# Graph attention layer: two heads' features in the two halves of the array, denominators as products of 32 columns

## The chip, the core and the metric

The kernel runs on one core of a Trainium2 chip. The metric is the device time of one execution in microseconds (us). TensorE multiplies, VectorE (DVE), ScalarE (ACT) and GpSimd (POOL) work element by element, and SyncE (SP) issues most transfers.

## What is computed

Four layers of a graph network run one after the other on 3125 nodes of 256 features. The change touches only the last one, graph attention with 4 heads of 64 features:

```python
ft = (feat @ W.T).reshape(n, HEADS, OUT_DIM)
a1 = jnp.einsum('nhd,hd->nh', ft, attn_l)
a2 = jnp.einsum('nhd,hd->nh', ft, attn_r)
e = jax.nn.leaky_relu(a1[src] + a2[dst], negative_slope=ALPHA)
m = jax.ops.segment_max(e, dst, num_segments=n)
ex = jnp.exp(e - m[dst])
s = jax.ops.segment_sum(ex, dst, num_segments=n)
msg = ft[src] * (ex / s[dst])[:, :, None]
out = jax.ops.segment_sum(msg, dst, num_segments=n)
return jax.nn.elu(out.reshape(n, HEADS * OUT_DIM))
```

For every head and target node this is a weighted sum of 64 features over the sources, and one more sum, of the weights alone, by which it is divided.

## The kernel before

Earlier layers build a dense matrix of edge counts, 25 by 25 blocks of 128 by 128 in bf16. The attention layer (`l3_fast`, from L2015) uses it in place of gathers. The targets are cut into ranges of up to 7 blocks (`RANGES`), and the layer runs 9 passes (`PASSES`, L1924), each for one pair of heads `i` and one range: four ranges for heads 0 and 1, five for heads 2 and 3. A pass has 25 steps `k`, one for each block of 128 sources.

In a step, for each head `u` of the pair, VectorE makes a tile of weights `wgt` (L2185), 128 sources by all targets of the range, in fp32, from the counts `cj`, a row `ratio` and a scalar for each source. TensorE multiplies it (L2234): the stationary operand is `ftx[:, k, head, :]`, 65 columns, which are 64 features and a column of scale factors whose product is the denominator; the moving operand is `wgt`. A range of more than 512 targets is cut into two pieces. So a step of a wide pass has 4 matmuls in the program, 2 heads by 2 pieces, and the five-block or smaller range has 2. Each fp32 matmul of the program appears in the trace as two weight loads and two matmuls on the same columns and the same output. They accumulate in `acc[p % 2][u]`, 65 partitions of two PSUM banks for each head; two passes alternate.

`wgt` has `NW = 3` buffers. VectorE waits for `m`, which TensorE raises after each head's matmuls (L2236), and TensorE waits for `w`. When a pass ends, ScalarE copies the accumulators to `oT` (L2109), TensorE turns them back at step 3 of the next pass (`turn`, L2214), and VectorE divides at its step 6 (`divide`, L2131) and, for the second pair of heads, applies the end of the layer (L2153 to L2164). GpSimd and VectorE scale `ftx` once ahead of the first pass (L2085, L2127). In the first pass TensorE also turns 25 small blocks (`row`, L2204).

Of the kernel before, what the change touches and what calls it, by code (L numbers as in the profile page):

```python
# [19 lines left out]
P = 128  # L20
N = 3125
# [1993 lines left out]
def l3_fast(nc, sem, sb, a, f, out):  # L2015
# [8 lines left out]
    with ExitStack() as ctx:  # L2024
        def buf(name, shape, dt=F32):
            return sb(name, shape, dt, ctx)
        NW, NC, FIRST = 3, 4, 3
        MOST = RANGES[0][1]
        UPPER = [p for p, (i, r) in enumerate(PASSES) if i]
        qs, e2, ng = buf("l3q", [P, NT, H]), buf("l3e2", [P, NT, H]), buf("l3ng", [P, H])  # L2030
# [1 line left out]
        rb = buf("ratio", [P, H, NP])  # L2032
        wgt = buf("wgt", [P, NW, 2, MOST * P])
        cj = buf("fcj", [P, NC, MOST, P], BF16)
        oT = buf("oT", [P, 2, MOST * P])
        den, rden = buf("fden", [P, 2, MOST]), buf("frden", [P, 2, MOST])
        neg = buf("fneg", [P, MOST, D])
        o = hx[:, :, 0:D]
        acc = [[psum[:, 4 * b + 2 * u:4 * b + 2 * u + 2, :] for u in range(2)] for b in range(2)]
        pR = psum[:, 4:6, :]  # L2040
        width = lambda r: min(N, (RANGES[r][0] + RANGES[r][1]) * P) - RANGES[r][0] * P
        half = lambda r: -(-width(r) // 2)
        pieces = lambda r: [(0, width(r))] if width(r) <= 512 else [(0, half(r)), (half(r), width(r))]
        span = lambda r: slice(RANGES[r][0], RANGES[r][0] + RANGES[r][1])
        ROWS_AT, TURN_AT, DIVIDE_AT, FINISH_AT, STORE_AT = 6, 3, 6, 10, 16
        WIDE_AT = (17, 20)
# [34 lines left out]
        @block.gpsimd  # L2081
        def _(eng):
            eng.wait_ge(s_("exp"), 2)
            for k in range(FIRST, NT):
                eng.tensor_tensor(ftx[:, k, :, :], ftx[:, k, :, :], e2[:, k, :].unsqueeze(2).to_broadcast([P, H, FW]), ALU.mult)\  # L2085
                   .then_inc(s_("ft"), 1)

        @block.scalar
        def _(eng):
            eng.wait_ge(s_("z"), 1)  # L2090
            eng.activation(qs[:, :, :], rr[:, :, 0:H], ACT.Exp, scale=0.8).then_inc(s_("exp"), 1)  # L2091
            eng.activation(e2[:, :, :], rr[:, :, 0:H], ACT.Exp, scale=0.2).then_inc(s_("exp"), 1)
            nt = RANGES[0][1]
            for u in range(2):
                eng.activation(rb[:, u, 0:nt * P], acc[0][u].rearrange("p b n -> p (b n)")[:, 0:nt * P], ACT.Exp,  # L2095
                               bias=ng[:, u:u + 1], scale=-0.8).then_inc(s_("rbp"), 1)
            eng.activation(rr[:, :, H:2 * H], rr[:, :, H:2 * H], ACT.Exp, scale=-0.8).then_inc(s_("exp"), 1)
            for g in range(7):
                w = min(4, NT - 4 * g) * P
                eng.wait_ge(s_("rowed"), g + 1)  # L2100
                eng.activation(rsb[:, 4 * g * P:4 * g * P + w], pR[0:H, g % 2, 0:w], ACT.Copy).then_inc(s_("rows"), 1)
            for p, (i, r) in enumerate(PASSES):
                nb = len(pieces(r))
                n = pieces(r)[0][1]
                eng.wait_ge(s_("m"), 2 * NT * (p + 1))
                if p:
                    eng.wait_ge(s_("turned"), p)
                for u in range(2):
                    last = eng.activation(oT[0:FW, u, 0:nb * n].rearrange("p (b n) -> p b n", b=nb), acc[p % 2][u][0:FW, 0:nb, 0:n], ACT.Copy)  # L2109
                    last.then_inc(s_("oT"), 1)  # L2110
                if i:
                    eng.wait_ge(s_("neg"), UPPER.index(p) + 1)
                    eng.activation(neg[:, 0:RANGES[r][1], :], neg[:, 0:RANGES[r][1], :], ACT.Exp).then_inc(s_("elu"), 1)

        @block.vector
        def _(eng):
# [7 lines left out]
            eng.wait_ge(s_("exp"), 2)  # L2124

            def scaled(k):
                eng.tensor_tensor(ftx[:, k, :, :], ftx[:, k, :, :], e2[:, k, :].unsqueeze(2).to_broadcast([P, H, FW]), ALU.mult)\  # L2127
                   .then_inc(s_("ft_first"), 1)
            scaled(0)

            def divide(p):  # L2131
# [2 lines left out]
                short = t0 + nt == NT  # L2134
                whole = nt - 1 if short else nt
                eng.wait_ge(s_("turned"), p + 1)
                sums = [acc[p % 2][u][:, 0, 0:nt * FW].rearrange("p (t f) -> p t f", f=FW) for u in range(2)]
                parts = [(P, 0, whole)] + ([(N - (NT - 1) * P, whole, nt)] if short else [])
                for u in range(2):
                    for q, lo, hi in parts:  # L2140
                        ch.do(eng.tensor_scalar(den[0:q, u, lo:hi], sums[u][0:q, lo:hi, HD], 1e-37, None, ALU.max))  # L2141
                ch.after()
                for q, lo, hi in parts:
                    ch.do(eng.reciprocal(rden[0:q, :, lo:hi], den[0:q, :, lo:hi]))  # L2144
                ch.after()
                for u in range(2):
                    for q, lo, hi in parts:
                        ch.do(eng.tensor_tensor(o[0:q, t0 + lo:t0 + hi, HD * (2 * i + u):HD * (2 * i + u + 1)], sums[u][0:q, lo:hi, 0:HD],  # L2148
                                                rden[0:q, u, lo:hi].unsqueeze(2).to_broadcast([q, hi - lo, HD]), ALU.mult))
                ch.after()  # L2150
                eng.sem_inc(s_("ev"), 1)
                if i:
# [13 lines left out]
            for p, (i, r) in enumerate(PASSES):  # L2166
# [4 lines left out]
                for k in range(NT):  # L2171
# [8 lines left out]
                    for u in range(2):  # L2180
                        if n == 0:
                            eng.wait_ge(s_("rbp"), u + 1)
                        if n >= NW:
                            eng.wait_ge(s_("m"), 2 * (n - NW) + u + 1)
                        eng.scalar_tensor_tensor(out=wgt[:, n % NW, u, 0:w], in0=rb[:, 2 * i + u, t0 * P:t0 * P + w],  # L2185
                                                 scalar=qs[:, k, 2 * i + u:2 * i + u + 1],
                                                 in1=here.rearrange("p k d -> p (k d)")[:, 0:w],
                                                 op0=ALU.max, op1=ALU.mult).then_inc(s_("w"), 1)
# [6 lines left out]
        def _(eng):  # L2195
# [11 lines left out]
            def turn(p):  # L2207
                r = PASSES[p][1]
                t0, nt = RANGES[r]
                eng.wait_ge(s_("oT"), 2 * p + 2)  # L2210
                for u in range(2):
                    for t in range(nt):
                        q = min(P, N - (t0 + t) * P)
                        last = eng.transpose(acc[p % 2][u][0:q, 0, t * FW:(t + 1) * FW], oT[0:FW, u, t * P:t * P + q], ident[0:FW, 0:FW])  # L2214
                last.then_inc(s_("turned"), 1)
            for p, (i, r) in enumerate(PASSES):
                if p == 1:
                    eng.wait_ge(s_("rows"), 7)
                if p > 1:
                    eng.wait_ge(s_("ev"), p - 1)  # L2220
                for k in range(NT):
# [6 lines left out]
                        eng.wait_ge(s_("ft_first"), k + 1)  # L2228
                    elif p == 0:
                        eng.wait_ge(s_("ft"), k - FIRST + 1)  # L2230
                    for u in range(2):
                        eng.wait_ge(s_("w"), 2 * n + u + 1)
                        for b, (lo, hi) in enumerate(pieces(r)):
                            last = eng.matmul(acc[p % 2][u][0:FW, b, 0:hi - lo], ftx[:, k, 2 * i + u, :], wgt[:, n % NW, u, lo:hi],  # L2234
                                              start=k == 0, stop=k == NT - 1, skip_group_check=True)
                        last.then_inc(s_("m"), 1)  # L2236
            turn(len(PASSES) - 1)


# [281 lines left out]
```

## Time and profile before

| | |
|---|---|
| median of 3 runs | 2154.23 us (2144.46 to 2157.07) |
| the profiled execution, its own time | 2139.71 us |
| its span, first to last instruction | 2137.8 us |
| mean granted clock of TensorE | 0.914 |
| span of the attention layer's 9 passes, first to last of the L2234 matmuls | 1582.0 to 2121.5 us |

In the trace "PE" is TensorE's matmuls, "PEld" its weight loads, and Ln is a line of the kernel. A matmul's duration includes the way through the array, so durations of successive matmuls overlap; the distance between two starts, called a slot here, is what each costs in a row of them. The same holds for VectorE to a smaller degree. "Busy" in the tables counts overlapped time once, "mean ns" does not.

### The profile page before, as it was taken

What the parts mean: (1) busy time and instruction counts of PE and PEld (TensorE: products, weight loads), DVE (VectorE), ACT (ScalarE), POOL (GpSimd) and SP (SyncE); (2) the same over time, 40 slices, a digit from 0 to 9 for tenths busy, and PEclk for the clock granted to TensorE, in tenths of its full rate; (3) what the DMA queues carried; (4) which work ended last, traced back from release to release, by engine and by line L of the source; (5) the groups of instructions that cost most, each with busy time, mean ns of one, the idle gap of its engine ahead of it and who ended that gap; (6) DMA issues with size and microseconds to landing.
All of it is one profiled execution on the core that took longest, in us unless ns stands there. A gap on an engine that the chain in (4) does not pass through costs nothing. (4 is left out here: it accounts for less than half of the span.)

```text
span 2137.8 us, 22846 instructions
## 1 busy us (share of the span) xinstructions
PE 1862.9 (87%) x7207; PEld 1136.3 (53%) x7207; DVE 1305.1 (61%) x1926; ACT 507.0 (24%) x738; POOL 1078.9 (50%) x1646
## 2 busy tenths in 40 slices
PE   3868967789979888988766999999889999999996
PEld 1246742266656555656554756778753444434443
DVE  5976758845524343443423565665587788878887
ACT  0500020034543434434333534200240000000000
POOL 3888888888888888888888700000032000000000
PEclk8955569899999999999888999999899999999998
DMA  9788850015544534443423432487223333434432
GB/s 352 316 323 338 323 187 23 9 36 182 185 138 140 167 110 156 151 155 135 143 93 139 155 114 81 147 300 227 93 48 91 89 81 86 102 89 106 96 83 69
DMA packets 335681, 313.04 MB, mean 146 GB/s; under 512 B 274432, under 2 KB 320234, under 8 KB 325867
## 3 DMA queue, kind: packets, MB, share of 16 engines
q1 hardware_dynamic: 220153, 265.90, 36.8%
q10 hardware_dynamic: 89654, 45.29, 7.2%
q0 software_dynamic: 25792, 0.88, 1.0%
q8 instruction: 36, 0.59, 0.1%
q14 instruction: 46, 0.38, 0.1%
HBM read 180.44 MB, written 131.55 MB: 146 GB/s over the span
## 5 line engine op out<-in xcount | busy, mean ns | idle before, releaser
L409 POOL DMA_INDIRECT table<-valT,idxT x806 | 777.5, 965 | 174.7 <-issue 139.9
L2234 PE MATMUL psum<-wgt,big 128*65 128x384 f32 (+4 forms) x1600 | 530.7, 493 | 8.6 <-DVE wgt L2185 8.5
L2185 DVE SCALAR_TENSOR_TENSOR wgt<-ratio,l3q,fcj 128x768 f32<-128x768 f32 (+4 forms) x442 | 408.0, 947 | 90.1 <-PE psum L2234 84.1
L2234 PEld LDWEIGHTS psum<-wgt,big 128*65 128x65 f32 x1600 | 219.4, 138 | 310.6 <-issue 283.9
L905 PE MATMUL psum<-hx,region 128*128 128x257 f32 x1250 | 303.9, 388 | 35.8 <-issue 28.5
L905 PE MATMUL psum<-region,g 128*128 128x512 f32 (+1 forms) x672 | 282.5, 566 | 1.5 <-DVE big L683 1.5
L905 PEld LDWEIGHTS psum<-hx,region 128*128 128x128 f32 x1250 | 229.7, 193 | 77.7 <-issue 39.5
L683 DVE TENSOR_TENSOR big<-big,psum 128x512 f32<-128x512 f32 (+1 forms) x325 | 209.5, 664 | 96.3 <-PE psum L905 65.4
L407 POOL MEMSET rest<- 128x256 f32 x805 | 264.4, 328 | 1.1 <-DMA table<-valT,idxT 0.6
L905 PEld LDWEIGHTS psum<-region,g 128*128 128x128 f32 x672 | 124.5, 195 | 126.7 <-issue 109.8
L1153 POOL PARTITION_ALL_REDUCE edges<-edge x1 | 0.5, 515 | 351.9 <-DVEq L1530 351.9
L849 ACT ACTIVATE region<-psum 128x512 f32<-128x512 f32 (+1 forms) x175 | 90.9, 551 | 357.3 <-PE psum L1004 250.9
L905 PE MATMUL psum<-tk,hx 128*128 128x100 bf16 x806 | 146.2, 357 | 22.2 <-DVE tk L629 21.4
L1238 PE MATMUL psum<-l2both,l2z 128*128 128x512 f32 (+1 forms) x700 | 147.6, 371 | 3.3 <-DVE l2z L1419 3.3
L905 PEld LDWEIGHTS psum<-tk,hx 128*128 128x128 bf16 x806 | 115.4, 145 | 52.7 <-DVE tk L629 24.7
L1004 PE MATMUL psum<-ident,tk 128*128 128x128 f32 x625 | 99.1, 292 | 47.7 <-DMA tk<-table 46.8
L1238 PEld LDWEIGHTS psum<-l2both,l2z 128*128 128x128 f32 x700 | 128.1, 189 | 22.2 <-DVE l2z L1419 4.1
L1385 DVE TENSOR_TENSOR l2both<-l2m 128x2560 fp32r<-128x2560 bf16 (+1 forms) x35 | 88.8, 2537 | 65.4 <-PE psum L1238 59.7
L1004 PEld LDWEIGHTS psum<-ident,tk 128*128 128x128 f32 x625 | 94.0, 206 | 52.9 <-DMA tk<-table 47.4
L2109 ACT ACTIVATE oT<-psum 65x768 f32<-65x768 f32 (+4 forms) x18 | 12.4, 741 | 449.5 <-PE psum L2234 449.5
L528 DVE TENSOR_TENSOR big<-psum,big 128x2048 bf16<-128x2048 f32 x48 | 109.4, 2289 | 12.6 <-ACT psum L801 7.9
L686 DVE TENSOR_TENSOR region<-region,ident 128x128 f32 (+1 forms) x24 | 7.0, 293 | 159.5 <-ACT region L874 154.5
(250 smaller groups left out, 1656.6 us busy)
## 6 DMA issues: line engine op xcount, KB each, us to landing
table<-tk SPq DMA_DIRECT2D x25, 3200.0 KB
tk<-table SPq DMA_DIRECT2D x25, 1664.0 KB
tk<-table SPq DMA_DIRECT2D x25, 1536.0 KB
fcj<-counts_b SPq DMA_DIRECT2D x125, 192.0 KB, 2.6
counts_t<-region ACTq DMA_DIRECT2D x25, 800.0 KB
counts_b<-region ACTq DMA_DIRECT2D x25, 800.0 KB
table<-valT,idxT POOLq DMA_INDIRECT x806
l2m<-counts_b SPq DMA_DIRECT2D x20, 640.0 KB, 5.4
```

Of the source, the lines that this page charges most:

```text
L407: eng.memset(rest[:, :], 0.0).then_inc(sem("rest"), 1)
L409: eng.indirect_dma_start(out=table, out_offset=bass.IndirectOffsetOnAxis(idxT[:, c:c + 1], 0), in_=valT[:, c, :], in_offset=None).then_inc ...
L528: eng.tensor_tensor(out, kbp[:, s, :].unsqueeze(1).unsqueeze(1).to_broadcast([P, 2, SB, P]), overlap(win[:, s, :, SB * m:SB * m + P]), ALU ...
L683: eng.tensor_tensor(part, part, more, ALU.add).then_inc(sem("af"), 1)
L849: eng.activation(cs[:, 4 * g:4 * g + w, :].rearrange("p j d -> p (j d)"), pC[:, g % 3, 0:w * P], ACT.Copy)\
L905: mm = lambda o, l, r_, st, sp: eng.matmul(o, l, r_, start=st, stop=sp, skip_group_check=True)
L1004: last = eng.transpose(pC[:, g % 3, o:o + P], tk[:, s, j, :, 0], ident[:, :])
L1238: mm = lambda o, l, r_, st, sp: eng.matmul(o, l, r_, start=st, stop=sp, skip_group_check=True)
L1385: eng.tensor_tensor(all_of(both[:, n % 2, :, :, :]), all_of(ca[n % NB]), all_of(cb[n % NB]), ALU.add).then_inc(s_("sum"), 1)
L2109: last = eng.activation(oT[0:FW, u, 0:nb * n].rearrange("p (b n) -> p b n", b=nb), acc[p % 2][u][0:FW, 0:nb, 0:n], ACT.Copy)
L2185: eng.scalar_tensor_tensor(out=wgt[:, n % NW, u, 0:w], in0=rb[:, 2 * i + u, t0 * P:t0 * P + w], scalar=qs[:, k, 2 * i + u:2 * i + u + 1], ...
L2234: last = eng.matmul(acc[p % 2][u][0:FW, b, 0:hi - lo], ftx[:, k, 2 * i + u, :], wgt[:, n % NW, u, lo:hi], start=k == 0, stop=k == NT - 1, ...
```

## The change

The two heads of a pass are multiplied on disjoint columns of the array: 64 features of head 0 write partitions 0 to 63, those of head 1 partitions 64 to 127 of the same bank (`product`). The denominators are no longer a 65th column. They are products of their own (`total`): the stationary operand is one column of scale factors repeated 32 times, and each of the four combinations of head and piece writes a quarter of 32 partitions of one bank, `sums`. `total` is called in every second step, for that step and the one before, and once alone in step 24. The banks, the copies (`oT` and a new `dT`), the transposes and the division follow the new layout, the pieces are cut at whole blocks, and `NW` goes from 3 to 5, since `m` now rises only after `total`. The scaling of `ftx` leaves the 65th column out. The wait for `rows` at pass 1 goes, since `pR` has banks of its own.

```diff
-        NW, NC, FIRST = 3, 4, 3
+        NW, NC, FIRST = 5, 4, 3
...
-        oT = buf("oT", [P, 2, MOST * P])
+        oT, dT = buf("oT", [P, MOST * P]), buf("dT", [P, 4 * P])
...
-        acc = [[psum[:, 4 * b + 2 * u:4 * b + 2 * u + 2, :] for u in range(2)] for b in range(2)]
-        pR = psum[:, 4:6, :]
+        flat = lambda t: t.rearrange("p b n -> p (b n)")
+        acc = [psum[:, 3 * b:3 * b + 2, :] for b in range(2)]
+        sums = [psum[:, 3 * b + 2, :] for b in range(2)]
+        scores_at = [flat(psum[:, 2 * u:2 * u + 2, :]) for u in range(2)]
+        pR = psum[:, 6:8, :]
-        half = lambda r: -(-width(r) // 2)
-        pieces = lambda r: [(0, width(r))] if width(r) <= 512 else [(0, half(r)), (half(r), width(r))]
+        half = lambda r: (RANGES[r][1] + 1) // 2
+        pieces = lambda r: [(0, width(r))] if width(r) <= 512 else [(0, half(r) * P), (half(r) * P, width(r))]
...
-                eng.tensor_tensor(ftx[:, k, :, :], ftx[:, k, :, :], e2[:, k, :].unsqueeze(2).to_broadcast([P, H, FW]), ALU.mult)\
+                eng.tensor_tensor(ftx[:, k, :, 0:HD], ftx[:, k, :, 0:HD], e2[:, k, :].unsqueeze(2).to_broadcast([P, H, HD]), ALU.mult)\
...
-                for u in range(2):
-                    last = eng.activation(oT[0:FW, u, 0:nb * n].rearrange("p (b n) -> p b n", b=nb), acc[p % 2][u][0:FW, 0:nb, 0:n], ACT.Copy)
-                    last.then_inc(s_("oT"), 1)
+                for bank, (lo, hi) in enumerate(pieces(r)):
+                    eng.activation(oT[:, lo:hi], acc[p % 2][:, bank, 0:hi - lo], ACT.Copy).then_inc(s_("oT"), 1)
+                eng.activation(dT[:, 0:n], sums[p % 2][:, 0:n], ACT.Copy).then_inc(s_("dT"), 1)
...
-                sums = [acc[p % 2][u][:, 0, 0:nt * FW].rearrange("p (t f) -> p t f", f=FW) for u in range(2)]
+                first = -(-pieces(r)[0][1] // P)
+                feats = flat(acc[p % 2])[:, 0:nt * P].rearrange("p (t u f) -> p t u f", u=2, f=HD)
+                totals = sums[p % 2].rearrange("p (t u b c) -> p b u t c", u=2, b=2, c=P // 4)
                 parts = [(P, 0, whole)] + ([(N - (NT - 1) * P, whole, nt)] if short else [])
-                for u in range(2):
+                for bank in range(len(pieces(r))):
                     for q, lo, hi in parts:
-                        ch.do(eng.tensor_scalar(den[0:q, u, lo:hi], sums[u][0:q, lo:hi, HD], 1e-37, None, ALU.max))
+                        lo, hi = max(lo, bank * first), min(hi, bank * first + first)
+                        if lo < hi:
+                            ch.do(eng.tensor_scalar(den[0:q, :, lo:hi], totals[0:q, bank, :, lo - bank * first:hi - bank * first, 0], 1e-37, None, ALU.max))
                 ch.after()
                 for q, lo, hi in parts:
                     ch.do(eng.reciprocal(rden[0:q, :, lo:hi], den[0:q, :, lo:hi]))
                 ch.after()
-                for u in range(2):
-                    for q, lo, hi in parts:
-                        ch.do(eng.tensor_tensor(o[0:q, t0 + lo:t0 + hi, HD * (2 * i + u):HD * (2 * i + u + 1)], sums[u][0:q, lo:hi, 0:HD],
-                                                rden[0:q, u, lo:hi].unsqueeze(2).to_broadcast([q, hi - lo, HD]), ALU.mult))
+                for q, lo, hi in parts:
+                    ch.do(eng.tensor_tensor(o[0:q, t0 + lo:t0 + hi, 2 * HD * i:2 * HD * i + 2 * HD].rearrange("p t (u f) -> p t u f", u=2), feats[0:q, lo:hi, :, :],
+                                            rden[0:q, :, lo:hi].rearrange("p u t -> p t u").unsqueeze(3).to_broadcast([q, hi - lo, 2, HD]), ALU.mult))
                 ch.after()
                 eng.sem_inc(s_("ev"), 1)
...
                         if n >= NW:
-                            eng.wait_ge(s_("m"), 2 * (n - NW) + u + 1)
+                            eng.wait_ge(s_("m"), 2 * (n - NW) + 2)
                         eng.scalar_tensor_tensor(out=wgt[:, n % NW, u, 0:w], in0=rb[:, 2 * i + u, t0 * P:t0 * P + w],
...
             def turn(p):
                 r = PASSES[p][1]
                 t0, nt = RANGES[r]
-                eng.wait_ge(s_("oT"), 2 * p + 2)
-                for u in range(2):
-                    for t in range(nt):
-                        q = min(P, N - (t0 + t) * P)
-                        last = eng.transpose(acc[p % 2][u][0:q, 0, t * FW:(t + 1) * FW], oT[0:FW, u, t * P:t * P + q], ident[0:FW, 0:FW])
+                r = PASSES[p][1]
+                eng.wait_ge(s_("oT"), sum(len(pieces(PASSES[e][1])) for e in range(p + 1)))
+                for t in range(nt):
+                    q = min(P, N - (t0 + t) * P)
+                    eng.transpose(flat(acc[p % 2])[0:q, t * P:(t + 1) * P], oT[:, t * P:t * P + q], ident[:, :])
+                eng.wait_ge(s_("dT"), p + 1)
+                n = pieces(r)[0][1]
+                for lo in range(0, n, P):
+                    last = eng.transpose(sums[p % 2][0:min(P, n - lo), lo:lo + P], dT[:, lo:min(n, lo + P)], ident[:, :])
                 last.then_inc(s_("turned"), 1)
+
+            def product(p, k):
+                i, r = PASSES[p]
+                for bank, (lo, hi) in enumerate(pieces(r)):
+                    for u in range(2):
+                        eng.matmul(acc[p % 2][HD * u:HD * u + HD, bank, 0:hi - lo], ftx[:, k, 2 * i + u, 0:HD], wgt[:, (NT * p + k) % NW, u, lo:hi],
+                                   start=k == 0, stop=k == NT - 1, skip_group_check=True)
+
+            def total(p, steps):
+                i, r = PASSES[p]
+                for k in steps:
+                    for u in range(2):
+                        for bank, (lo, hi) in enumerate(pieces(r)):
+                            at = P // 4 * (2 * u + bank)
+                            last = eng.matmul(sums[p % 2][at:at + P // 4, 0:hi - lo], e2[:, k, 2 * i + u:2 * i + u + 1].to_broadcast([P, P // 4]),
+                                              wgt[:, (NT * p + k) % NW, u, lo:hi], start=k == 0, stop=k == NT - 1, skip_group_check=True)
+                last.then_inc(s_("m"), 2 * len(steps))
             for p, (i, r) in enumerate(PASSES):
-                if p == 1:
-                    eng.wait_ge(s_("rows"), 7)
...
-                    for u in range(2):
-                        eng.wait_ge(s_("w"), 2 * n + u + 1)
-                        for b, (lo, hi) in enumerate(pieces(r)):
-                            last = eng.matmul(acc[p % 2][u][0:FW, b, 0:hi - lo], ftx[:, k, 2 * i + u, :], wgt[:, n % NW, u, lo:hi],
-                                              start=k == 0, stop=k == NT - 1, skip_group_check=True)
-                        last.then_inc(s_("m"), 1)
+                    eng.wait_ge(s_("w"), 2 * n + 2)
+                    product(p, k)
+                    if k % 2:
+                        total(p, (k - 1, k))
+                    elif k == NT - 1:
+                        total(p, (k,))
             turn(len(PASSES) - 1)
```

Not shown: ScalarE's first reads of the scores go by `scores_at`, the same banks as before, and the second scaling line (L2127) changes as the first.

## Rows read from the trace of the kernel before

**Rows 1.** The page's part 1, TensorE's entry: busy us, share, instructions.

```profile
PE 1862.9 (87%) x7207; PEld 1136.3 (53%) x7207; DVE 1305.1 (61%) x1926; ACT 507.0 (24%) x738; POOL 1078.9 (50%) x1646
```

**Rows 2.** Chain that ended last, from 1575 us to the end: shares by line.

```profile
by line: PE psum L2234 90.3%; DVE wgt L2185 2.0%; PE psum L2214 1.1%; issue 0.7%; DVE xs L2156 0.7%; DVE xs L2164 0.6%; DVE fneg L2153 0.5%; PE psum L2204 0.5%; DVE hx L2148 0.4%; ACT ratio L2095 0.2%; DVE fden L2141 0.1%; ACT oT L2109 0.1%
```

**Rows 3.** Windows: a wide pass (384 targets a piece), then the two narrow ones.

```profile
core 0: us, PE busy (x) PEld busy (x) DVE busy (x) ACT busy (x) POOL busy (x), PEclk, DMA share, GB/s
...
1662.00:1727.30 65.30, 65.30 (x215) 28.42 (x214) 52.17 (x55) 1.72 (x2) 0.00 (x0) 1.00 0.37 87
...
2058.40:2093.80 35.40, 33.42 (x113) 14.35 (x112) 32.65 (x58) 2.99 (x3) 0.00 (x0) 1.00 0.41 100
2093.80:2121.70 27.90, 26.85 (x107) 13.82 (x105) 24.79 (x54) 1.71 (x3) 0.00 (x0) 1.00 0.36 86
```

**Rows 4.** Groups by form, 1580 to 2138 us: the product's matmuls (347 is as 346).

```profile
L2234 PE MATMUL psum<-wgt,big 128*65 128x384 f32 x900 | 291.8, 486 | 2.0 <-DVE wgt L2185 2.0
...
L2234 PE MATMUL psum<-wgt,big 128*65 128x448 f32 x400 | 154.2, 545 | 5.5 <-DVE wgt L2185 5.5
...
L2234 PE MATMUL psum<-wgt,big 128*65 128x346 f32 x100 | 37.4, 455 | 0.0
...
L2234 PE MATMUL psum<-wgt,big 128*65 128x309 f32 x100 | 26.8, 424 | 1.1 <-DVE wgt L2185 0.9
```

**Rows 5.** Timeline of TensorE, a few matmuls of each width: start, us, instruction.

```profile
1699.43 1.45 PE L2234 MATMUL psum<-wgt,big 128*65 128x384 f32 x4
...
1879.72 1.67 PE L2234 MATMUL psum<-wgt,big 128*65 128x448 f32 x4
...
1819.78 1.62 PE L2234 MATMUL psum<-wgt,big 128*65 128x346 f32 x5
...
2109.76 1.46 PE L2234 MATMUL psum<-wgt,big 128*65 128x309 f32 x5
```

**Rows 6.** Timeline around 1701 us: two weight loads one slot apart.

```profile
1701.37 0.14 PEld L2234 LDWEIGHTS psum<-wgt,big 128*65 128x65 f32 x1 [0.18 <-issue]
1701.69 0.14 PEld L2234 LDWEIGHTS psum<-wgt,big 128*65 128x65 f32 x1 [0.18 <-issue]
```

**Rows 7.** Waits, 1582 to 2122 us: who for whom, us in total, times, longest.

```profile
DVE wgt L2185 <- PE psum L2234: 84.1, 277, 0.9
...
PE psum L2234 <- DVE wgt L2185: 8.5, 4, 5.5
```

**Rows 8.** Groups, 1580 or 1582 to 2138 us: VectorE's weight tiles (442 and 8).

```profile
L2185 DVE SCALAR_TENSOR_TENSOR wgt<-ratio,l3q,fcj 128x768 f32<-128x768 f32 x200 | 200.8, 1017 | 45.8 <-PE psum L2234 45.3 <-DVE hx L2148 0.4
...
L2185 DVE SCALAR_TENSOR_TENSOR wgt<-ratio,l3q,fcj 128x768 f32<-128x768 f32 (+4 forms) x442 | 408.0, 947 | 90.1 <-PE psum L2234 84.1 <-DMA fcj<-counts_b 4.1 <-DVE hx L2148 0.9
...
L2185 DVE SCALAR_TENSOR_TENSOR wgt<-ratio,l3q,hx 128x896 f32<-128x896 f32 x8 | 9.8, 1279 | 0.5 <-ACT ratio L2095 0.5
```

**Rows 9.** Timeline of VectorE, three weight tiles made without a wait between them.

```profile
1943.72 2.87 DVE L2185 SCALAR_TENSOR_TENSOR wgt<-ratio,l3q,fcj 128x768 f32<-128x768 f32 x3
```

**Rows 10.** Groups of VectorE, 1582 to 2138 us: its larger work beside the weights.

```profile
L2148 DVE TENSOR_TENSOR hx<-psum,frden 128x384 f32<-128x384 f32 (+5 forms) x22 | 8.9, 453 | 0.3
...
L2156 DVE SCALAR_TENSOR_TENSOR xs<-hx,xs 128x1536 f32<-128x1536 f32 (+2 forms) x5 | 7.5, 1492 | 0.8 <-DVE fneg L2153 0.8
L2164 DVE SCALAR_TENSOR_TENSOR xs<-fneg,xs 128x1536 f32<-128x1536 f32 (+2 forms) x5 | 7.4, 1487 | 0.0
L2153 DVE TENSOR_SCALAR fneg<-hx 128x1536 f32<-128x1536 f32 (+2 forms) x5 | 5.8, 1169 | 0.7
```

**Rows 11.** Timeline of TensorE in the first pass: small transposes between products.

```profile
1602.26 0.60 PE L2204 MATMUL psum<-ident,small 128*4 128x128 f32 x4
1602.70 3.17 PE L2234 MATMUL psum<-wgt,big 128*65 128x448 f32 x8
```

**Rows 12.** The chain in order of time (start, us, what), around a turn.

```profile
1670.02 0.87 PE psum L2214 x14
1670.89 64.50 PE psum L2234 x200
```

More of the change, by code:

```diff
@@ L2094, in _ @@
             for u in range(2):
-                eng.activation(rb[:, u, 0:nt * P], acc[0][u].rearrange("p b n -> p (b n)")[:, 0:nt * P], ACT.Exp,
+                eng.activation(rb[:, u, 0:nt * P], scores_at[u][:, 0:nt * P], ACT.Exp,
                                bias=ng[:, u:u + 1], scale=-0.8).then_inc(s_("rbp"), 1)
@@ L2102, in _ @@
             for p, (i, r) in enumerate(PASSES):
-                nb = len(pieces(r))
                 n = pieces(r)[0][1]
@@ L2126, in scaled @@
             def scaled(k):
-                eng.tensor_tensor(ftx[:, k, :, :], ftx[:, k, :, :], e2[:, k, :].unsqueeze(2).to_broadcast([P, H, FW]), ALU.mult)\
+                eng.tensor_tensor(ftx[:, k, :, 0:HD], ftx[:, k, :, 0:HD], e2[:, k, :].unsqueeze(2).to_broadcast([P, H, HD]), ALU.mult)\
                    .then_inc(s_("ft_first"), 1)
```

## Prediction, made before the kernel with the change was run

> **What bounds the kernel now.** I read the page's busy times first, then the chain of waits for the stretch of the attention layer, then that stretch by windows, groups and timeline. TensorE is the busiest engine of the whole kernel, 87% [rows 1]. In the stretch that the change touches, from 1575 us to the end, 90.3% of the chain is the matmuls of L2234 and only 2.0% VectorE's weight tiles [rows 2]. In a wide pass TensorE is busy for all of 65.30 us and VectorE for 52.17, at a granted clock of 1.00, which is 2.4 GHz [rows 3]. VectorE waits 84.1 us for those matmuls, in 277 waits, and TensorE only 8.5 us for VectorE, in four [rows 7]. So TensorE's slots set the length of the layer, and VectorE is the next limit.
>
> What a slot is: four matmuls of 384 columns take 1.45 us, one of them 0.486 [rows 4, 5], so a start follows a start after (1.45 - 0.486) / 3 = 0.321 us. In the same way 448 columns cost (1.67 - 0.545) / 3 = 0.375, 346 cost (1.62 - 0.455) / 4 = 0.291, and 309 cost (1.46 - 0.424) / 4 = 0.259 us. A weight load starts one slot after the one before it and lasts 0.14 us [rows 6], so it lies under a running matmul and costs nothing.
>
> The layer in slots: 900 x 0.321 + 400 x 0.375 + 200 x 0.291 + 100 x 0.259 = 288.9 + 150.0 + 58.2 + 25.9 = 523 us. 100 of the 900 and the 100 of 309 columns are the two narrow passes, 58 us; the seven wide passes have 1400 matmuls, 465 us. The layer's matmuls run from 1582.0 to 2121.5 us, 539.5 us, so 16.5 us is starts, transposes and waits. All sums are made against the profiled execution's own 2139.7 us; the median of the runs shown is 14.5 us above it, and I add what I find to the median.
>
> **The change part by part.**
>
> *How many matmuls.* The width of the stationary operand does not enter a slot: 65 columns take 0.321 us for 384 moving columns, which is 2 x 384 clocks at 2.4 GHz and nothing for the 65. So 64 columns cost the same, and the separate denominators double the number: 2800 in the wide passes for 1400, 400 in the narrow ones for 200. In series that would be 523 us more. All now depends on how much of it runs at the same time on different columns of the array, and no row of before has two matmuls at once. The bounds are one at a time, 523 us more, and as many as there are disjoint column ranges, two in `product` and four in `total`.
>
> *What I take for the overlap.* Each fp32 matmul of the program is two in the trace, on the same columns (A A', then for the other head B B'). A' needs A's columns, so it starts one slot after A. In the rows every matmul starts after the one before it in program order. If TensorE keeps to that order, B cannot pass the waiting A', and starts with it. Then B' and the next A start together, and so on: a chain in which two run at once, never more, and whose end adds one slot. For `product` of two wide steps, 16 matmuls, that gives 8 + 1 slots. For `total` of the same two steps, again 16 matmuls in pairs, on four quarters in turn, it gives also 8 + 1, since the third quarter is blocked behind the second half of the second just as well. Before, two steps took 16 slots. So with an order that is kept the four quarters bring no more than the two halves, and the work per slot is exactly what it was.
>
> *The end of each group.* Whether the 1 is paid depends on whether halves and quarters may run at once. Below: not at all, if the quarters start as soon as their columns are free; then `total` begins in the slot in which `product`'s last pair ends, and nothing is lost. The nearest rows are the first pass's small transposes: four of them and then eight products start without a gap [rows 11], but these all use the array as one piece. Above: the array runs empty at each change, then the chain's extra slot is paid and the matmul's way out too, 0.486 - 0.321 = 0.165 us, and at worst a weight load of 0.14 us that nothing covers. I take the extra slot and the way out without the load, since the halves and quarters are different divisions of the same columns and the load can be under way while the last matmul drains. The Trainium skill says so of the first part (TensorEngine Tiling (Array Packing), Tiling Modes, Key Properties): a change of the tiling mode, not of the tile alone, drains TensorE. By it the sum is the one below; without it this item is zero. No run here shows it yet.
>
> *The sum.* A wide pass: twelve pairs of steps at 18 slots and the last step at 5 + 5, 226 slots for 200, so 0.13 x 465 = +60.5 us. A narrow pass has 8 matmuls in `product` of two steps, so 5 + 5 for 8, and 3 + 3 for the last step: 126 for 100, 0.26 x 58 = +15.1 us. Changes between halves and quarters: 13 groups x 2 x 9 passes = 234, at 0.165 us +38.6 us.
>
> *The small parts.* `turn` has 11 transposes for 14 (7 + 4) in the first pass, but their moving side is 128 wide: four such take 0.44 us [rows 11], 0.11 each, so 1.2 us where 14 now take 0.87 [rows 12]; nine passes give about +2.3 us. The copies on ScalarE cover fewer columns and lie beside the next pass's matmuls, except the last; the division has fewer instructions and is off the path while VectorE has room. In the two narrow passes 35.4 + 27.9 = 63.3 us [rows 3] stand against 58 of slots: VectorE's divisions hold TensorE there; a slower TensorE hides about 3 us of it, -3. `NW = 5` covers the later release: two buffers belong to the pair that runs, three more steps are ready, and VectorE refills two in 4 x 0.93 = 3.7 us, while TensorE takes 18 slots, 5.8 us. The wait for both heads' weights in place of one is hidden for the same reason, as is the coarser `m`. The scaling of `ftx` and the wait for `rows` are at most some tenths of a us.
>
> Together 60.5 + 15.1 + 38.6 + 2.3 - 3 = +113.5 us: 2139.7 + 113.5 = 2253 for a profiled execution, and 2154.2 + 113.5 = 2268 as a median. With the uncovered loads it is 234 x 0.138 = 32 more, 2300.
>
> **The rivals.**
>
> *A, full overlap, faster.* TensorE holds a waiting matmul for each range of columns, so that B starts with A and all four quarters run at once. A pair of wide steps is then 8 + 4 slots, a wide pass 150 for 200: -0.25 x 465 = -116 us. A narrow pass has only two quarters in use and is even. With the drains (38.6) and `turn` it is -75, 2079 us. Without the drains TensorE would ask for 2154 - 114 = 2040, but now VectorE stops it. Its 442 tiles x 0.947 + 8 x 1.279 = 429 us [rows 8] less an overlap of 1.017 - (2.87 - 1.017) / 2 = 0.09 each [rows 9], so 389 us, with 29.6 us of the rows beside [rows 10] and some 5 us of small ones: 423 us for 539.5. Since each pass goes by the slower of the two, I take about -105, 2049 us. For it speaks that disjoint columns share nothing but the order; against it that every start in the trace follows program order. It decides from the point at which a pair of steps takes less than 16 slots with its drains. The Trainium skill (TensorE: Matmul & The Clock Gate, Part 3, Measured speedup vs the span model) gives 2.38 times for three column tiles; taken over to both parts that would be this rival. The same part says that matmuls start and end strictly in order, which is my forecast's side. Neither measured two in a row on one tile.
>
> *B, order kept but no drain: no change.* 16 slots for 16, with +2.3 and some stalls hidden: 2154 us, 2140 to 2165. For it: the rows without a gap [rows 11].
>
> *C, little or no overlap, much slower.* If weight loads wait for the column range before them, each A to B passage shows a load; if nothing overlaps, the layer costs 523 us more, 2677 us. Anything above 2300 is here.
>
> **How the numbers follow.** Forecast 0.37 (2230 to 2300), A 0.34 (2040 to 2085), B 0.14, C 0.13, rest 0.02. The forecast is the likeliest, 2268. The range 2040 to 2300 leaves out C and the rest; it holds both signs, the forecast's own is 2230 to 2300. About 1% is what a measurement can tell from no change: faster 0.34, same 0.15, slower 0.51.
>
> **What would show it.** In the profile after, the timeline of a wide pass: starts of matmuls in pairs, one slot between pairs, in both lines, and after each group a gap of about 0.165 us and no start for a slot; 5.8 to 6.1 us for two steps where 5.15 stand now; VectorE waiting for TensorE more than 84 us. Four starts within 0.02 us in `total` would refute the order and give A. `product`'s last and `total`'s first matmul side by side give B. Starts never together give C. If VectorE is busy without a wait in the wide passes, the layer is near A's lower end.

## The result and the profile after

The kernel with the change takes 2086.94 us (median of 4 runs, 2078.43 to 2087.63), the kernel before 2149.35 us beside it (4 runs). The ratio is 0.9701, with a 95% interval of 0.9652 to 0.9749: 3% faster, some 62 us. The forecast was 2268 us and slower. Rival A, full overlap, had 2079 us with the drains, and a range of 2040 to 2085.

Windows of the changed kernel, over the same three passes as [rows 3] (columns as there) and one pass of the second pair of heads:

```profile
1669.10:1722.60 53.50, 53.50 (x413) 19.45 (x411) 48.48 (x55) 1.47 (x3) 0.00 (x0) 1.00 0.46 108
...
1890.30:1946.50 56.20, 54.05 (x413) 19.25 (x411) 53.72 (x58) 3.17 (x4) 0.00 (x0) 1.00 0.49 118
...
2001.00:2039.40 38.40, 37.48 (x213) 11.36 (x209) 31.85 (x57) 2.74 (x4) 0.00 (x0) 1.00 0.39 96
2039.50:2070.80 31.30, 30.93 (x208) 11.13 (x206) 23.75 (x50) 1.75 (x4) 0.00 (x0) 1.00 0.31 73
```

The wide pass of 65.30 us is now 53.50, with twice the matmuls (x413 for x215) and the same granted clock. The narrow passes went the other way, 38.4 + 31.3 for 35.4 + 27.9 us. The layer's matmuls run from 1600.3 to 2070.3 us: 470.0 us for 539.5, 69.5 less.

The span of this profiled execution is only 51.9 us shorter (2085.9 for 2137.8), since the layer began 18 us later, at 1600.3 for 1582.0. No run shows that the change does this: in the seven runs below on chips of like speed the layer begins between 1588 and 1600 us, and in the one of them that is the kernel before with more buffers at 1599.3.

Timeline of TensorE, changed kernel, inside the second pass (start, us, instruction):

```profile
1691.41 2.80 PE L2230 MATMUL psum<-wgt,big 128*64 128x384 f32 x16
1694.14 1.50 PE L2239 MATMUL psum<-wgt,l3e 128*32 128x384 f32 x16
1695.57 2.80 PE L2230 MATMUL psum<-wgt,big 128*64 128x384 f32 x16
1698.30 1.50 PE L2239 MATMUL psum<-wgt,l3e 128*32 128x384 f32 x16
```

A pair of steps repeats every 1695.57 - 1691.41 = 4.16 us. From the first of the 16 products to the first of the next line it is 2.73 us, which is two at a time (8 slots are 2.58), and for the 16 denominators' products 1.43 us, four at a time (4 slots are 1.29). So what is beyond 12 slots, 3.87 us, is 0.29 us, or 0.145 on average for each change between halves and quarters. In the single records the products start in pairs, 6 to 7 ns apart, the second pair 0.374 us after the first and each further one 0.322 us after the one before, and the denominators in fours, again 6 to 7 ns from one to the next.

Groups by form, changed kernel:

```profile
L2230 PE MATMUL psum<-wgt,big 128*64 128x384 f32 x1200 | 224.5, 495 | 3.6 <-DVE wgt L2190 3.4
...
L2239 PE MATMUL psum<-wgt,l3e 128*32 128x384 f32 x1200 | 150.1, 492 | 0.0
```

The waits of the layer, changed kernel (who for whom, us, times, longest):

```profile
PEld psum L2230 <- DVE wgt L2190: 62.0, 102, 1.7
...
DVE wgt L2190 <- PE psum L2239: 29.1, 51, 1.8
...
PE psum L2230 <- DVE wgt L2190: 10.5, 10, 6.6
DVE fden L2147 <- PE psum L2223: 10.1, 9, 5.5
```

One matmul of 384 columns still lasts about 0.49 us, as in [rows 4]. What changed is how many run at once. VectorE waits 29.1 us for TensorE's products instead of the 84.1 of [rows 7], and TensorE's loads now wait 62.0 us for VectorE. Before, that was 15.5 us:

```profile
PEld psum L2234 <- DVE wgt L2185: 15.5, 54, 2.1
```

A waiting load costs nothing while matmuls run. In the wide pass of 53.50 us TensorE is still busy all the time, and VectorE for 48.48; in the second pair's pass of 56.20 us VectorE is busy for 53.72, and TensorE, with 54.05, has gaps. So TensorE still sets the first pair's passes, with VectorE close behind, and VectorE's extra work in the second pair's now holds TensorE up.

### The profile page after: what moved, and what is told of

It is laid out like the page before. It is cut to its first block and busy times, and to the rows that moved or that the text cites. A ratio compares the mean times of both kernels' runs of the same rounds, so it can differ in the third digit from the quotient of the medians.

```text
span 2085.9 us, 25985 instructions
## 1 busy us (share of the span) xinstructions
PE 1769.4 (85%) x8777; PEld 1080.1 (52%) x8786; DVE 1285.5 (62%) x1911; ACT 502.8 (24%) x745; POOL 1082.0 (52%) x1646
## 3 DMA queue, kind: packets, MB, share of 16 engines
q1 hardware_dynamic: 220153, 265.90, 37.6%
## 5 line engine op out<-in xcount | busy, mean ns | idle before, releaser
L2190 DVE SCALAR_TENSOR_TENSOR wgt<-ratio,l3q,fcj 128x768 f32<-128x768 f32 (+4 forms) x442 | 388.2, 950 | 35.4 <-PE psum L2239 29.1
L2230 PE MATMUL psum<-wgt,big 128*64 128x384 f32 (+2 forms) x1600 | 294.2, 502 | 10.8 <-DVE wgt L2190 10.5
L905 PE MATMUL psum<-region,g 128*128 128x512 f32 (+1 forms) x672 | 270.1, 547 | 1.0 <-DVE big L683 1.0
L1004 PE MATMUL psum<-ident,tk 128*128 128x128 f32 x625 | 106.3, 308 | 173.2 <-DMA tk<-table 172.4
L905 PEld LDWEIGHTS psum<-hx,region 128*128 128x128 f32 x1250 | 235.8, 197 | 31.7 <-ACT region L849 0.6
L2230 PEld LDWEIGHTS psum<-wgt,big 128*64 128x64 f32 x1600 | 103.4, 137 | 196.1 <-issue 127.8
L1004 PEld LDWEIGHTS psum<-ident,tk 128*128 128x128 f32 x625 | 99.4, 208 | 180.2 <-DMA tk<-table 174.3
L2239 PE MATMUL psum<-wgt,l3e 128*32 128x384 f32 (+2 forms) x1600 | 176.2, 497 | 0.0
L905 PEld LDWEIGHTS psum<-tk,hx 128*128 128x128 bf16 x806 | 116.1, 144 | 37.9 <-DVE tk L629 10.1
## 6 DMA issues: line engine op xcount, KB each, us to landing
tk<-table SPq DMA_DIRECT2D x25, 1664.0 KB, 10.1
```

What stands on the lines that cost most here:

```text
L905: mm = lambda o, l, r_, st, sp: eng.matmul(o, l, r_, start=st, stop=sp, skip_group_check=True)
L1004: last = eng.transpose(pC[:, g % 3, o:o + P], tk[:, s, j, :, 0], ident[:, :])
L2230: eng.matmul(acc[p % 2][HD * u:HD * u + HD, bank, 0:hi - lo], ftx[:, k, 2 * i + u, 0:HD], wgt[:, (NT * p + k) % NW, u, lo:hi], start=k == ...
L2239: last = eng.matmul(sums[p % 2][at:at + P // 4, 0:hi - lo], e2[:, k, 2 * i + u:2 * i + u + 1].to_broadcast([P, P // 4]), wgt[:, (NT * p + ...
```

## The experiments

The number to compare is the layer's, from its first matmul to its last, in one profiled execution each: 539.5 us before, 470.0 with the change. Seven runs were on chips on which the kernel before takes 2146 to 2156 us. The other five (the products in rows of eight, the denominators on halves, the later division, the narrow passes and the last one) were on chips on which it takes 2332 to 2333 us, so their whole times are only comparable with the kernel before beside them; with 384 columns the rhythm of the changed code, 4.157 us, is the same there. Where no ratio is given, the kernel was timed in one execution only, and the argument goes by its rhythm and its layer.

### Which order do the matmuls start in

The forecast rested on this. Two runs alter the order in which the program gives the matmuls.

> The changed kernel with one edit: in a step, head 0's matmuls for both pieces come ahead of head 1's, where they alternated by head. Theory P (parking): a matmul whose columns are busy is set aside, one for each range of columns, and the next in program order goes on; only a second one for the same columns blocks. Then head 1 lags head 0 by two slots at the start of each product, and a pair of wide steps takes 10 + 4 slots for 8 + 4: with 384 columns a period of 4.157 + 0.645 = 4.80 us, the layer about 470 + 45 = 515 us. Theory D (deep): many wait for each range of columns: the period stays 4.157 us and the layer 470 us. Theory O (strict order, with the two passes of the fp32 matmul interleaved by head in the instruction stream): four in a row on the same columns run one by one, no pair starts together within a step, period about 16 slots for the product, 6.7 us, layer over 600 us.

```diff
-                for bank, (lo, hi) in enumerate(pieces(r)):
-                    for u in range(2):
+                for u in range(2):
+                    for bank, (lo, hi) in enumerate(pieces(r)):
                         eng.matmul(acc[p % 2][HD * u:HD * u + HD, bank, ...
```

> The changed kernel with one edit: in the denominators' products the two steps are the innermost loop, so that four matmuls of the trace in a row go to one quarter, then four to the next. Theory P: each quarter lags the one before by two slots, 10 slots for 4, period 4.157 + 6 x 0.322 = 6.1 us. Theory D: 4 slots as now, period 4.157 us. Theory O: about one by one, 16 slots, 8 us.

```diff
-                for k in steps:
-                    for u in range(2):
-                        for bank, (lo, hi) in enumerate(pieces(r)):
+                for u in range(2):
+                    for bank, (lo, hi) in enumerate(pieces(r)):
+                        for k in steps:
```

Timeline of TensorE, head outermost:

```profile
1690.82 2.85 PE L2230 MATMUL psum<-wgt,big 128*64 128x384 f32 x16
1693.60 1.50 PE L2239 MATMUL psum<-wgt,l3e 128*32 128x384 f32 x16
1695.02 2.85 PE L2230 MATMUL psum<-wgt,big 128*64 128x384 f32 x16
```

The same, denominators in runs of four to one quarter:

```profile
1697.85 2.80 PE L2230 MATMUL psum<-wgt,big 128*64 128x384 f32 x16
1700.58 1.52 PE L2239 MATMUL psum<-wgt,l3e 128*32 128x384 f32 x16
1702.02 2.80 PE L2230 MATMUL psum<-wgt,big 128*64 128x384 f32 x16
```

The periods are 4.20 and 4.17 us where parking a single matmul would have given 4.80 and 6.1, and the layers 474.3 and 472.2 us. With four matmuls in a row for the same columns, those for other columns still start within the same slot: the quarters 13 to 14 ns apart instead of 6 to 7, the halves 13 to 14 ns at first and up to 57 ns towards the end of a line. Both the strict order of the forecast and the parking of one are out. The third run lengthens the row to eight.

> The changed kernel with the products of both steps of a pair made together, head 0's eight matmuls of the trace ahead of head 1's eight. Theory, a long list for each range of columns: the halves still run together, head 1 starts about 8 x 0.0065 = 0.05 us after head 0, a period of 4.2 to 4.3 us. If a list holds about four, head 1 lags by four slots and the period is 4.157 + 1.3 = 5.4 us. Beside this TensorE now starts the product only when the second step's weights are there, which costs up to 1.87 us a pair where VectorE is not ahead.

```diff
-                for bank, (lo, hi) in enumerate(pieces(r)):
-                    for u in range(2):
+                for u, k in [(u, k) for u in range(2) for k in steps]:
+                    for bank, (lo, hi) in enumerate(pieces(r)):
...
-                    product(p, k)
                     if k % 2:
+                        product(p, (k - 1, k))
                         total(p, (k - 1, k))
                     elif k == NT - 1:
+                        product(p, (k,))
                         total(p, (k,))
```

Timeline of the weight loads, one for each matmul, this kernel:

```profile
1883.68 0.19 PEld L2230 LDWEIGHTS psum<-wgt,big 128*64 128x64 f32 x2 [0.62 <-issue]
1884.06 0.14 PEld L2230 LDWEIGHTS psum<-wgt,big 128*64 128x64 f32 x1 [0.19 <-issue]
1884.38 0.14 PEld L2230 LDWEIGHTS psum<-wgt,big 128*64 128x64 f32 x1 [0.18 <-issue]
1884.70 0.14 PEld L2230 LDWEIGHTS psum<-wgt,big 128*64 128x64 f32 x1 [0.19 <-issue]
1885.03 0.84 PEld L2230 LDWEIGHTS psum<-wgt,big 128*64 128x64 f32 x7 [0.18 <-issue]
1886.05 0.14 PEld L2230 LDWEIGHTS psum<-wgt,big 128*64 128x64 f32 x1 [0.18 <-issue]
1886.38 0.14 PEld L2230 LDWEIGHTS psum<-wgt,big 128*64 128x64 f32 x1 [0.19 <-issue]
```

Timeline of its matmuls:

```profile
1883.68 4.14 PE L2230 MATMUL psum<-wgt,big 128*64 128x384 f32 x16
1887.76 1.50 PE L2239 MATMUL psum<-wgt,l3e 128*32 128x384 f32 x16
1889.18 4.14 PE L2230 MATMUL psum<-wgt,big 128*64 128x384 f32 x16
```

Here is the limit. Single loads, a slot apart, stand at the front, then seven within 0.84 us, which are those of both heads side by side, and single ones again at the end. A record does not name its head; by the order in the program, head 0's first four matmuls run alone, the fifth together with head 1's first, 5 ns apart, and head 1's last four alone. So head 1 lags by four slots, and the 16 products take 12 slots: 4.08 us to the next line for 2.73. The layer takes 581.1 us, 111 more than with the change. The period is 5.50 us, 4.157 + 4 slots + 0.05, as the expectation had for "about four". When the fifth starts, three are left for the same columns, and the program goes on past them; with seven left it had not. In the head-outermost run the three behind the first did not block either. So beside the running one, three may wait for the same columns. The count goes by range of columns and not by the whole: with the denominators in runs of four, the fourth quarter's first matmul starts 40 ns after the first quarter's, while nine others wait, three for each of the quarters ahead of it. Whether the limit counts matmuls or loads was not tried.

### Is it the overlap that saves the time

> The changed kernel with one edit: both heads' features are multiplied on partitions 0 to 63 (head 1's sums fall on head 0's, so the output is not the reference's). If overlap of the two halves is what saved the time, the product takes 16 slots for 8 and its starts come one by one, 0.322 us apart: a period of 4.157 + 2.58 = 6.7 us, the layer about 740 us. If the time came from the later release, the buffers or the narrower stationary operand, the layer stays near 470 us.

```diff
-                        eng.matmul(acc[p % 2][HD * u:HD * u + HD, bank, ...
+                        eng.matmul(acc[p % 2][0:HD, bank, ...
```

Timeline of TensorE:

```profile
1714.56 1.50 PE L2239 MATMUL psum<-wgt,l3e 128*32 128x384 f32 x16
1715.99 5.37 PE L2230 MATMUL psum<-wgt,big 128*64 128x384 f32 x16
1721.29 1.50 PE L2239 MATMUL psum<-wgt,l3e 128*32 128x384 f32 x16
```

Yes. With both heads on the same columns 16 products take 5.30 us for 2.73, the period is 6.73 us and the layer 725.3 us. Everything else is as in the changed kernel, so the two halves for the products alone are worth 255 us in it. The quarters still go four at a time.

### What a change between halves and quarters costs

> The changed kernel with one edit: the denominators' products come in every step, so halves and quarters change 50 times a pass and not 26. Theory: each change costs what the rhythm of the changed kernel shows, (4.157 - 12 x 0.322) / 2 = 0.145 us, whatever stands between. Then 24 more changes a pass, 216 x 0.145 = +31 us less what VectorE held back before: +25 to +31 us. Rival: a change costs nothing and the 0.29 us of a period is waiting for VectorE: 0 us.

```diff
-                    if k % 2:
-                        total(p, (k - 1, k))
-                    elif k == NT - 1:
-                        total(p, (k,))
+                    total(p, (k,))
```

> The changed kernel with the denominators' products on the two halves, 64 columns wide, in place of quarters (the sums of the two pieces of a wide pass fall on each other, so its output is not the reference's). The division of the array never changes. Theory: the gap of 0.416 us for a slot of 0.322 at each switch comes from the change of division and goes; the denominators take 8 slots for 4: a period of 16 x 0.322 = 5.15 us with 384 columns, the layer about 470 + 100 = 570 us. Rival: the gap comes from the other line's weights or bank and stays, period 5.4 us.

```diff
-                            at = P // 4 * (2 * u + bank)
-                            last = eng.matmul(sums[p % 2][at:at + P // 4, ...], e2[...].to_broadcast([P, P // 4]), ...
+                            at = HD * u
+                            last = eng.matmul(sums[p % 2][at:at + HD, ...], e2[...].to_broadcast([P, HD]), ...
```

Timeline of TensorE, denominators in every step:

```profile
1700.32 1.51 PE L2230 MATMUL psum<-wgt,big 128*64 128x384 f32 x8
1701.76 0.85 PE L2239 MATMUL psum<-wgt,l3e 128*32 128x384 f32 x8
1702.54 1.51 PE L2230 MATMUL psum<-wgt,big 128*64 128x384 f32 x8
```

The same, denominators on halves:

```profile
1861.26 2.80 PE L2239 MATMUL psum<-wgt,l3e 128*64 128x384 f32 x16
1863.84 2.80 PE L2230 MATMUL psum<-wgt,big 128*64 128x384 f32 x16
1866.42 2.80 PE L2239 MATMUL psum<-wgt,l3e 128*64 128x384 f32 x16
```

In every step the period is 2.22 us, 6 slots (1.93) and again 0.29 us for two changes. The layer is 496.4 us, +26.4 for 216 changes, which at 0.145 us are 31; that the rest had been waiting for VectorE before, as the expectation has it, is likely and not shown. With the array divided in one way only, a line follows the other after exactly 8 slots, 2.58 us, and the period is 5.16: nothing beyond the slots. So the 0.145 us belongs to the change of division and to nothing else. That layer is 546.0 us and not 570, because the changes that it saves were not in my round number: 50 slots more in each of seven wide passes are 116 us, 234 changes fewer 34, together +82 for the measured +76. A pair then takes 16 slots, as in the kernel before, whose layer was 539.5 us: halves for everything gain nothing, and the gain of the change lies in the quarters.

### The buffers

> The kernel before with five weight buffers for three and nothing else. TensorE set the pace in the wide passes and VectorE's extra lead covers only the divisions in the narrow ones: 0 to -3 us. If the buffers were a part of the gain, it would be -10 us or more.

```diff
-        NW, NC, FIRST = 3, 4, 3
+        NW, NC, FIRST = 5, 4, 3
```

> The changed kernel with three weight buffers for five. Two belong to the pair of steps that runs, so VectorE is one step ahead at most. It makes step k+1 while k's pair runs and the next two only after the denominators' products: TensorE waits about one step's weights, 1.87 us less the 1.29 us of a product, in each pair: +0.6 to +1.9 us in each of some 108 pairs, +60 to +150 us. Rival: VectorE's lead does not matter, 0 us.

```diff
-        NW, NC, FIRST = 5, 4, 3
+        NW, NC, FIRST = 3, 4, 3
```

The kernel before with five buffers: ratio 1.0002 (0.9979 to 1.0025), layer 538.9 us. By themselves they are worth nothing. The changed kernel with three: ratio to the kernel before 1.0097 (1.0059 to 1.0135), layer 567.6 us, 97.7 more than with five, inside the expected 60 to 150. Its timeline shows how:

```profile
1691.28 1.50 PE L2239 MATMUL psum<-wgt,l3e 128*32 128x384 f32 x16
1692.70 1.51 PE L2230 MATMUL psum<-wgt,big 128*64 128x384 f32 x8
1694.91 1.51 PE L2230 MATMUL psum<-wgt,big 128*64 128x384 f32 x8 [0.70 <-DVE wgt L2190]
1696.35 1.50 PE L2239 MATMUL psum<-wgt,l3e 128*32 128x384 f32 x16
```

One step's products, then 0.70 us idle for VectorE, then the second's. The products in pairs of steps need buffers that hold them: with three, the gain turns into a loss of 1%.

### What is left: fewer changes, the narrow passes, the division's place

> The changed kernel with the denominators' products in every third step (9 groups a pass for 13) and six buffers. Theory: 8 changes a pass fewer, 72 x 0.145 = 10 us; VectorE's own work is 423 us of the layer's 470, so it gives -5 to -10 us. Rival: VectorE holds TensorE already, 0 us.

```diff
-        NW, NC, FIRST = 5, 4, 3
+        NW, NC, FIRST = 6, 4, 3
...
-                    if k % 2:
-                        total(p, (k - 1, k))
+                    if k % 3 == 2:
+                        total(p, tuple(range(k - 2, k + 1)))
                     elif k == NT - 1:
-                        total(p, (k,))
+                        total(p, tuple(range(NT - NT % 3, NT)))
```

Ratio to the kernel before 0.9678 (0.9628 to 0.9728), layer 467.7 us: -2.3, less than the 5 to 10 expected. The period is 6.09 us for three steps, 2.03 for one instead of 2.08, so in the steady rhythm TensorE got what was due, and the rest went elsewhere. The trace also shows a wait that grew:

```profile
DVE fden L2147 <- PE psum L2223: 22.4, 9, 5.0
DVE wgt L2190 <- PE psum L2239: 16.5, 25, 1.9
```

VectorE comes to the division before TensorE has turned the sums: 22.4 us for 10.1. One wait of each, 5.0 and 5.5 us, is for the last division and lies behind the layer's last matmul. Inside the layer it is 17.4 us for 4.7.

> The changed kernel with the division at VectorE's step 9 for 6 and the end of the layer at 13 for 10. With five buffers VectorE comes to the division before TensorE has turned the sums, and waits 10.1 us in 9 waits, where before it was 3.9 in one. Theory: these waits go, the layer is 2 to 8 us shorter. Rival: TensorE is the slower one in those passes, and nothing changes.

```diff
-        ROWS_AT, TURN_AT, DIVIDE_AT, FINISH_AT, STORE_AT = 6, 3, 6, 10, 16
+        ROWS_AT, TURN_AT, DIVIDE_AT, FINISH_AT, STORE_AT = 6, 3, 9, 13, 18
```

A miss. The waits fell to 5.5 us in one, the one behind the layer, so the later division could save no more than the 4.7 us inside it, and not the 10.1 that the expectation had in view. The layer is 473.1 us, 3 more. VectorE's wait for free buffers rose from 29.1 to 37.6 us: what it no longer waits for at the division it waits for there, and more.

> The changed kernel with all four quarters in use in the two narrow passes: even and odd steps' denominators go to different quarters and are added at the division. A pair takes 2 slots for 4 there: 24 x (0.321 + 0.259) = 14 us less work for TensorE, of which VectorE's tiles (52 us with its divisions for the 69 us of the two passes) leave about 10: -8 to -14 us. If the narrow passes hang on VectorE alone: 0.

```diff
-                            at = P // 4 * (2 * u + bank)
+                            turns = 3 - len(pieces(r))
+                            at = P // 4 * (2 * u + (bank if turns == 1 else k % 2))
...
-    start=k == 0, stop=k == NT - 1, ...
+    start=k < turns, stop=k >= NT - turns, ...
```

and an addition of the two quarters ahead of the reciprocal. Windows of its two narrow passes:

```profile
2175.50:2210.80 35.30, 30.48 (x211) 8.49 (x209) 31.00 (x55) 2.62 (x5) 0.00 (x0) 1.00 0.41 100
2210.90:2238.20 27.30, 25.01 (x206) 7.97 (x202) 23.99 (x52) 1.84 (x4) 0.00 (x0) 1.00 0.37 88
```

35.3 + 27.3 us for 38.4 + 31.3, and the layer is 463.0 us, -7.0, just under the expected 8 to 14. VectorE is busy 31.0 of the 35.3 us there. The ratio to the kernel before beside it is 0.9665 (0.959 to 0.9741).

> Both edits that shortened the layer, together: the denominators' products in every third step with six buffers, and all four quarters in use in the narrow passes. If the two shorten it independently, the layer is 470.0 - 2.3 - 7.0 = 461 us against 539.5 before, a ratio of about 0.963 to the kernel before. If both draw on the same slack of VectorE: the layer stays at 463 us or above, the ratio at 0.966 or above.

The layer is 461.8 us, 8.2 less than with the change alone, against 461 if the two edits add up. So they do, nearly. The ratio to the kernel before, on one of the slower chips, is 0.9688 (0.9649 to 0.9728), 76 us of 2332. Its interval and that of the change, 0.9652 to 0.9749, overlap, and they were not measured on one chip: that this version beats the changed kernel is shown for the layer, in one profiled execution of each, and not for the whole time. The same holds for each of the two edits alone, whose intervals, 0.9628 to 0.9728 and 0.959 to 0.9741, overlap with it too.

## Why the prediction was wrong, step by step

- **What bounds the kernel.** Right. TensorE's slots set the layer and VectorE was next; now it is close behind (48.48 us of 53.50 in a wide pass). The slot of 0.322 us, independent of the stationary operand's width, held in each run.
- **The number of matmuls.** Right: 3200 for 1600.
- **The overlap.** Here it failed. "If TensorE keeps to that order, B cannot pass the waiting A', and starts with it." It can, as the runs above show. The rows had every start in program order, but in a kernel in which every matmul uses the same columns nothing else can be seen; I read the absence of an alternative as a rule. The price of that step: 26 slots too many in each wide pass where 50 fewer was true, 60.5 + 116 = 177 us, and 15 us in the narrow passes.
- **The drain.** Right in kind: a change of division costs 0.145 us on average, to the 0.165 taken from matmul duration less slot. The size agrees to 12%, but a way out of 0.165 us is not shown to be its cause: the start after a change comes 0.416 us after the last start, before that matmul's 0.486 us are over (its end is modelled), and another 0.05 us falls at the second start of the products and 0.02 at that of the denominators. The Trainium skill says (TensorEngine Tiling (Array Packing), Tiling Modes, Key Properties) that TensorE drains at each change of the tiling mode. These runs agree as far as a cost of 0.145 us stands at each change and is gone in the run on halves alone; that it is a drain they do not show.
- **The extra slot at a group's end.** Wrong with the overlap: there is no chain that lags, hence no end of one.
- **The small parts.** A turn of 7 blocks takes 1.36 us for 0.87, with 11 transposes at 0.12 us where 0.11 was taken. `NW = 5` hid the later release as said, and the run with three shows the cover's worth, 98 us.
- **Rival A's sum.** It had -75 us with the drains, the layer gave -69.5. The seven wide passes give -76.5 us and the narrow ones +6.2, each from its own first to its own last matmul (the gaps between passes grew by 0.9); A's terms give -116 + 30 + 2 = -84 and +9. Of the 7.7 us that the wide passes lack, about 7 are uneven pieces, as four quarters wait for the longest: with 512 and 384 columns a pair takes 5.005 us where 12 mean slots and two changes are 4.79, 25 pairs in the two passes, and 3.90 for 3.78 with 384 and 309; some 4 are put down to VectorE, whose divisions and end of the layer fall into the second pair of heads' passes (55.9 and 54.0 us for 53.1); the cheaper changes give some 4 back. That the quarters would be uneven stood in the diff, and I left it out.
- **The chances.** The right rival, A, had 0.34, the forecast 0.37. The Trainium skill's speedup of 2.38 for three column tiles (TensorE: Matmul & The Clock Gate, Part 3, Measured speedup vs the span model) spoke for A. The same part of the Trainium skill says that matmuls start strictly in order, on which I leaned as well; that is not what these runs show: in the run with rows of eight, head 1's first matmul starts with head 0's fifth, while three that stand ahead of it in the program still wait. The measurement decides.

## What to carry to other kernels

Narrow stationary operands (64 or 32 columns) placed on disjoint columns of the array run side by side even in fp32, two and four at a time, so where TensorE sets the pace, a product that leaves columns empty can be worth splitting, even if it takes twice the instructions. Count the slots first: with the denominators on halves a pair of steps took 16 slots, as before the change, and nothing was gained; on quarters it took 12. Order within a group hardly matters as long as no more than four in a row go to the same columns; make the pieces equal, and put off the other division of the array to a few changes, each 0.145 us. Count the buffers that the delay holds: with three for five the same change lost 1%.

## What the runs showed of the hardware that was not expected

- Matmuls for free columns pass those that wait for busy ones. Three may wait beside the running one for each range of columns; with eight in a row the other half started four slots late.
- Concurrent starts are 6 to 7 ns apart, and 13 to 14 ns when four in a row for one quarter stand between.
- Changing between halves and quarters costs 0.145 us a time on average, in groups of one, two and three steps alike; two lines on the same division follow each other at exactly one slot.
